# Moving the input normalisation of an attention loop from VectorE to ScalarE

## The reference

```python
x = x + tanh(g_xattn[0]) * attention(layernorm(x), ctx, ctx)   # 16 blocks of 128 tokens, 256 wide, 16 heads of 16
x = x + tanh(g_ffn[0]) * ffn(layernorm(x))                     # 32 experts x 4 sets, slots of 32 tokens

def _layernorm(x, eps=1e-05):
    m = jnp.mean(x, axis=-1, keepdims=True)
    v = jnp.var(x, axis=-1, keepdims=True)
    return (x - m) / jnp.sqrt(v + eps)
```

## Time and profile before

| | |
|---|---|
| median of three runs | 270.87 us |
| the profiled execution, in all | 272.54 us |
| its span, first to last instruction | 270.8 us |
| PE busy | 224.6 us, 83% |
| DVE busy | 199.5 us, 74% |
| ACT busy | 167.0 us, 62% |
| POOL busy | 129.2 us, 48% |
| mean granted clock of PE | 0.950 |

### The profile page before, as it was taken

One profiled execution on the slowest core, in us unless ns is written; L12 is line 12 of the kernel. 1 busy time (PEld: TensorE's weight loads), 2 busy tenths in 40 slices (PEclk: granted clock), 3 DMA queues, 4 the chain that ended last, 5 costly groups with the idle time before them and its releaser, 6 DMA issues.

```text
span 270.8 us, 7540 instructions
## 1 busy us (share of the span) xinstructions
PE 224.6 (83%) x2850; PEld 175.8 (65%) x2850; DVE 199.5 (74%) x454; ACT 167.0 (62%) x356; POOL 129.2 (48%) x243
## 2 busy tenths in 40 slices
PE   0465769499788799899989998979998999985994
PEld 0455668387576688687757676857786777773451
DVE  4786738669999969599698887789996555552573
ACT  2642648558657859778577766625887554456562
POOL 5632275555767568857586777654665000000000
PEclk9996868989999999999999999997999999997699
DMA  6735649833253442434310000007996387899724
GB/s 193 228 94 150 176 113 286 248 92 88 75 141 99 119 122 61 121 98 112 82 52 23 7 4 2 4 2 243 394 383 227 85 179 207 233 236 215 174 97 138
DMA packets 32230, 37.91 MB, mean 140 GB/s; under 512 B 4099, under 2 KB 27331, under 8 KB 31939
## 3 DMA queue, kind: packets, MB, share of 16 engines
q1 hardware_dynamic: 31763, 36.85, 47.8%
q10 hardware_dynamic: 432, 0.59, 0.9%
HBM read 18.26 MB, written 6.29 MB: 91 GB/s over the span
## 4 chain that ended last, share of the span: by engine, by line
PE 34%; DVE 19%; POOL 15%; issue 12%; DMA 8%; ACT 6%; SPq 5%; ACTq 0%; POOLq 0%; DVEq 0%
POOL pT L482 6%; PE banks L857 4%; DVE rsum L1268 4%; PE banks L931 4%; PE banks L712 4%; PE banks L732 4%; PE banks L916 3%; PE banks L754 3%; PE banks L875 3%; PE banks L603 3%; DVE nmax L1260 3%; SPq L299 2%; DMA y<-y_rows 2%; DMA w<-in_wattn_dram 2%; POOL xs L476 2%
## 5 line engine op out<-in xcount | busy, mean ns | idle before, releaser
L1260 DVE TENSOR_REDUCE nmax<-banks 128x4 f32<-128x512 f32 x64 | 43.7, 683 | 23.2 <-PE banks L666 22.9
L482 POOL TENSOR_SCALAR_AFFINE_SELECT pT<-pT 128x512 f32<-128x512 f32 x64 | 40.8, 638 | 39.3 <-ACT pT L1023 39.3
L1028 ACT ACTIVATE banks<-cb 128x512 f32<-128x512 bf16 x62 | 37.0, 597 | 12.3 <-DVE nmax L1260 12.2
L1023 ACT ACTIVATE pT<-banks 128x512 f32<-128x512 f32 x64 | 37.5, 586 | 7.5 <-PE banks L683 7.5
L683 PE MATMUL banks<-qst,kst 99*128 99x128 bf16 x256 | 25.8, 224 | 3.9 <-DMA qst<-nT 3.7
L1268 DVE RECIPROCAL rsum<-banks 128x256 f32<-128x256 f32 x16 | 28.0, 1748 | 1.3 <-PE banks L712 1.2
L712 PE MATMUL banks<-pT,va 128*32 128x128 f32 x512 | 27.4, 287 | 0.0
L666 PE MATMUL banks<-kst,qst 96*128 96x128 bf16 x256 | 25.9, 225 | 1.6 <-ACT banks L1028 1.6
L712 PE MATMUL banks<-pT,ones 128*32 128x128 f32 x512 | 25.8, 273 | 0.0
L683 PEld LDWEIGHTS banks<-qst,kst 99*128 99x128 bf16 x256 | 15.5, 100 | 9.1 <-DMA qst<-nT 3.9
L1108 ACT ACTIVATE routed<-banks 128x512 f32<-128x512 f32 x30 | 17.2, 628 | 5.3 <-PE banks L754 5.3
(11 more groups left out here) (133 smaller groups left out, 633.8 us busy)
## 6 DMA issues: line engine op xcount, KB each, us to landing
wx<-in_wexp_dram SPq DMA_DIRECT2D x32, 256.5 KB, 7.3
kst<-kp SPq DMA_DIRECT2D x48, 128.0 KB, 2.4
qst<-qp SPq DMA_DIRECT2D x48, 128.0 KB, 2.4
cT<-in_ctxT_dram SPq DMA_DIRECT2D x8, 256.0 KB, 3.4
y_rows<-ring SPq DMA_DIRECT2D x16, 128.0 KB, 3.3
y<-y_rows SPq DMA_DIRECT2D x4, 512.0 KB, 5.2
wx<-y_rows SPq DMA_DIRECT2D x4, 512.0 KB, 8.3
out_dram<-xs SPq DMA_DIRECT2D x16, 128.0 KB, 2.0
```

What stands on the lines that cost most here:

```text
L482: pool.affine_select(p, p, [[0, HC], [1, P]], ALU.is_ge, 0.0, base=0, channel_multiplier=-1)\
L1023: act.activation(pT[:, n % PR, :], BT[n % 2], ACT.Exp, scale=float(D) ** -0.5).then_inc(p_ready, 1)
L1028: act.activation(BS[n % 2], causal, ACT.Copy).then_inc(mask_placed, 1)
L1260: dve.tensor_reduce(nmax[:, b % 2, :].rearrange("p (e j o) -> p e o j", e=2, o=KH)[:, e, o], BS[n % 2].rearrange("p (j t) -> p j t", j=HC) ...
```

## The change

In the loop, DVE no longer normalises the 12 blocks 4 to 15. ACT does, in the same slots (s = 0 and 1), right behind its mask of the next chunk and ahead of its exponential. Its instruction computes `Identity(scale * x + bias)` with scale and bias read per token: the scale is the reciprocal deviation `rs`, the bias is minus mean times `rs`. DVE makes that bias for six, four and four blocks at once, with one small instruction behind each chain of deviations (`shift_x`). It is written into `ve`, which the chain no longer needs, and a new semaphore `shift_x_ready` tells ACT. The four blocks ahead of the loop and the second layernorm stay as they were.

```diff
+            def normalize_x(b):
+                act.wait_ge(shift_x_ready, 1 if b < 8 else b // 4)
+                act.wait_ge(xT_done, (b - 4) // 2 + 1)
+                act.activation(xn[:, b % 4, :], xs[:, b, :], ACT.Identity, bias=ve[:, b:b + 1], scale=rs[:, b:b + 1])\
+                    .then_inc(xn_ready, 1)
...
                 if 1 <= n < CH - 1:
                     place_mask(n + 1)
+                if s in (0, 1) and g + 2 < NG2:
+                    normalize_x(2 * (g + 2) + s)
...
-            def normalize_x(b):
-                if b >= 4:
-                    dve.wait_ge(xT_done, (b - 4) // 2 + 1)
-                normalize(b, xn_ready)
+            def shift_x(lo, hi):
+                rstd_ready(lo)
+                dve.scalar_tensor_tensor(ve[:, lo:hi], mv[:, lo:hi, 0], -1.0, rs[:, lo:hi], ALU.mult, ALU.mult)\
+                    .then_inc(shift_x_ready, 1)
...
-            normalize_x(2)
-            normalize_x(3)
+            normalize(2, xn_ready)
+            normalize(3, xn_ready)
+            shift_x(2, 8)
...
                 if n < CH:
                     row_max(n)
-                if s in (0, 1) and g + 2 < NG2:
-                    normalize_x(2 * (g + 2) + s)
                 if s == 1 and g + 2 < NG2:
                     k_rest(g + 2)
...
                     if n == first + 8:
-                        rstd_ready(lo)
+                        shift_x(lo, lo + 4)
```

More of the change, by code:

```diff
@@ L200, in build @@
         stats_ready = sem("stats_ready")
+        shift_x_ready = sem("shift_x_ready")
         tanh_ready = sem("tanh_ready")
@@ L1323, in _ @@
             rstd_ready(0)
-            normalize_x(0)
-            normalize_x(1)
+            normalize(0, xn_ready)
+            normalize(1, xn_ready)
             weight_low(Q)
```

## The result

The changed kernel takes 273.94 us (median of 19 runs, 271.86 to 276.36) against 271.33 us (19 runs, 269.55 to 273.59). The ratio is 1.0088, 95% interval 1.0062 to 1.0113, so about 2.4 us slower, 1.7 to 3.1. Every ratio in this document leaves out the runs more than 1.5% above the fastest of their kernel, which are 1 of 19 for the changed kernel but 7 of 12 in e3_copy and 7 of the 17 of the kernel before that stand beside e11 and e12, so a ratio can differ by up to 1% from what the medians of all runs say.

The account below looks back on a forecast made before the run. The prediction took a closed loop of waits through PE, DVE, ACT and POOL, 17.28 us a round, as the bound. Terms 2x - (1.63 - 2x) + 4x = 8x - 1.63, with x = 0.46, gave +2.05 us: 272.9 us, 8-in-10 range 270.3 to 274.2.

Parts of the forecast that it names:

- slower still: Rival: in round 3 masks or PE's transposes hold k_rest at its old time, nothing gained; 3.1 us slower, 274.0; chance 0.16.
- The loop through PE, ACT, DVE and POOL: Attention loop: a closed chain of waits, 17.28 us a round; a microsecond put into one link is a microsecond on the round.
- The step x: Time one added activation pushes back what follows it on ACT: 0.30 + 0.11 bias + 0.05 scale = 0.46 us, ends 0.30 and 0.52.
- Round 2: Attention loop: k_rest already waits for ACT's k_high, so the two added activations lengthen the round by 2x.
- Round 3: Attention loop: DVE came last to k_rest, so moving the normalisations gains 1.63 - 2x, with 0.28 us of ACT's delay absorbed.
- Rounds 4 and 5: Attention loop: k_rest waits for k_high, so +2x each; PE's transposes of the maxima 18.2 us apart in place of 17.28.
- Rounds 0 and 1 at nothing: Start of the loop: chain lies with SP's issues and the 4.01 us transfer of the maxima, so the added activations cost nothing.
- `shift_x` at nothing: Three small DVE bias instructions of about 0.16 us, costed at nothing under cover of other waits; 0.2 to 0.3 each if uncovered.
- PE's wait for the maxima: PE's wait before its transpose of the row maxima in rounds 4 and 5, about 1 us, was to become about 1.9 us.
- The masks: ACT's masks queued behind the new activations: PE uses them one or two slots later, so their delay stays inside that of k_high.
- The rival of the ports: Small DVE stages escape POOL's operations on the shared port pair; up to 3.4 us recovered, 269.5 us, kernel faster; chance 0.13.
- POOL and DVE move together: Argument against the port rival: the same DVE results set POOL's operations going through ACT, so the 0.06 us offset stays.

Follow-up runs that it names:

- e3_copy: Changed kernel with its twelve activations as plain copies, without scale and bias per token; ratio 0.9983 (0.9930 to 1.0035) against the kernel before.
- e11: Kernel before with ACT normalising only blocks 10 to 15, one slot before the round, ahead of the output's high part; ratio 0.9995 (0.9955 to 1.0036).
- e12: Kernel before with ACT normalising blocks 10 to 15 in its idle wait and k_high ahead of its slot's exponential and maxima copy; ratio 0.9828, median 266.79 us.
- e1: Changed kernel with ACT normalising only in rounds 4 and 5, DVE in rounds 0 to 3; ratio 1.0084 (1.0047 to 1.0120) against the kernel before.
- e4: Changed kernel with the two activations of rounds 1 to 5 moved right behind k_high on ACT; ratio 0.9944 (0.9906 to 0.9982) against the kernel before.
- e8: Changed kernel with activations behind k_high, and k_high ahead of its slot's exponential and maxima copy; ratio 0.9940 (0.9902 to 0.9979) against the kernel before.
- e10: Kernel before with k_high ahead of its slot's exponential and maxima copy, and both DVE normalisations in slot s = 0; ratio 0.9905 (0.9862 to 0.9948).
- e3b_bias: Changed kernel with the scale left out of the twelve activations, bias kept; one run, difference of medians +1.6 us against the kernel before.
- e6: Changed kernel with ACT normalising only in rounds 0 and 1, DVE in all others; ratio 1.0034 (1.0003 to 1.0066) against the kernel before.
- e9: Kernel before with only k_high taken ahead of the exponential and the copy of the maxima of its slot; ratio 0.9925 (0.9899 to 0.9951).
- e2: Changed kernel with ACT normalising only in round 3, DVE in all other rounds; ratio 0.9969 (0.9929 to 1.0008) against the kernel before.

## Why the prediction was right

The direction, the size (+2.05 forecast, about +2.4 measured) and the mechanism held. The median of 273.94 us lies inside the range of 8 in 10 but above the forecast's own range, which ended at 273.6; the kernel before was itself 0.46 us higher in this measurement (271.33 for 270.87). It is also next to the 274.0 of the rival "slower still", and there the number alone would mislead: that rival needed round 3 to gain nothing, and it gained 0.63. Point by point:

- **The loop through PE, ACT, DVE and POOL** held. e1 adds 0.98 us of ACT work to each of two rounds and they are 0.98 and 0.97 us longer. e11 adds the same work where ACT waits and it costs under 0.1. In rounds 3 to 5 the distance from `k_rest` to the next mark is 7.22 to 7.25 us in every kernel but e4, e8 and e10, so the time of such a round is set by when `k_rest` starts.
- **The step x** was the mis-sized term: 0.46 forecast, 0.49 measured. The bias was priced at 0.11 and costs 0.09; the scale was put at half of that and costs the whole 0.09. The estimate by the Trainium skill ("ScalarE: Activation LUTs", What ACT_TABLE_LOAD costs), 0.492, was the better one, and e3b_bias and e3_copy agree with its 93 ns for each operand (90 and 93). With x = 0.49 the sum is +2.29 against +2.39 by the marks.
- **Round 2** +2x: 0.92 forecast, +1.00. **Round 3** 1.63 - 2x: a gain of 0.71 forecast, 0.63; the 0.28 us that ACT was to absorb there are in the trace, where `onh` to `k_high` grew by 4.46 - 3.76 = 0.70 and not by 0.98. **Rounds 4 and 5** 18.2 us forecast, 18.29 and 18.28.
- **Rounds 0 and 1 at nothing** is not shown. e6 leaves between nothing and about 1 us for them, as said there.
- **`shift_x` at nothing** held for the last of the three, the only one between the marks. In the changed kernel it is short:

```profile
86.25 0.16 DVE L1205 SCALAR_TENSOR_TENSOR rs<-nt,rs 128x4 f32<-128x4 f32 x1
86.44 0.16 DVE L1229 SCALAR_TENSOR_TENSOR ve<-mv,rs 128x4 f32<-128x4 f32 x1
```

In e1 it is not, and there the nothing is partly luck. It took 0.55 us beside POOL's operations, and the normalisation behind it, so made later, took 0.74 in place of the 1.20 of before:

```profile
85.75 0.55 DVE L1229 SCALAR_TENSOR_TENSOR ve<-mv,rs 128x4 f32<-128x4 f32 x1
...
86.25 1.16 POOL L460 TENSOR_TENSOR qp<-qr,qp 128x512 bf16<-128x512 f32 x1
86.82 0.74 DVE L1223 TENSOR_SCALAR xn<-xs,mv,rs 128x256 f32<-128x256 f32 x1
```

- **One sign of it was wrong.** PE's wait for the maxima was to grow to about 1.9 us. It is 1.05. PE does lose the time, but it loses it earlier in the round, ahead of its transposes of x and of its projection of `onh`. Neither had a named wait in round 4 before:

```profile
107.88 0.66 PE L596 MATMUL banks<-cf,xn 128*128 128x128 f32 x4 [0.23 <-DVE kr L1246]
...
109.94 0.39 PE L626 MATMUL banks<-wh,onh 128*128 128x256 f32 x1 [0.39 <-ACT va L1016]
```

Counted from the mark, the transposes start 0.46 us later than before and the projection 0.96 us later, nearly all of the round's delay. The first waits for `k_rest`, the second for ACT's copy of the values, which also stands behind the two activations. The prediction had named neither. The masks, which it had named, did stay inside the delay of `k_high`: between the 4th and the 11th mark PE names no wait for them.

- **The rival of the ports** did not show in the changed kernel: the four slow small stages of DVE in round 2 took 1.12, 0.66, 0.58 and 1.23 us before and after. The fifth, 0.68 us at 85.08, did become 0.16 (86.25), but `k_high` came last there and nothing was gained by it. The argument against this rival, that POOL and DVE move together, is weaker than the prediction put it. In e9 moving one activation by 0.64 us separated them by 0.37 us and gave back 0.75.

## What to carry to other kernels

Before work is moved from a busy engine to a less busy one, look for the last arrival at the instruction where the two engines meet, round by round: here ACT was 62% busy overall and yet without any idle time in just the eight instructions ahead of `k_high`. The same work is nearly free where that engine's own row shows an idle wait (1.88 us ahead of `onh`; it cost 0.06 us a round in e11). And where two engines arrive together, as both did at `k_rest` in rounds 4 and 5, relieving either alone gave at most 0.06 us; the pair of edits gave 0.55.

## What the runs showed of the hardware that I had not expected

PE's granted clock fell once in the later part of the attention loop in the traces of six kernels and not in those of the other seven. Stretches of e4_behind and then of the kernel before:

```profile
134.50:136.50 2.00, 0.84 (x12) 0.45 (x8) 1.57 (x4) 2.00 (x5) 1.44 (x6) 1.00 0.04 8
136.00:138.00 2.00, 1.69 (x26) 1.07 (x24) 1.54 (x4) 1.92 (x5) 1.92 (x5) 0.72 0.49 131
138.00:140.00 2.00, 2.00 (x24) 1.39 (x23) 1.35 (x2) 1.20 (x2) 2.00 (x3) 0.50 0.03 6
```

```profile
136.00:138.00 2.00, 0.86 (x9) 0.52 (x9) 1.57 (x4) 2.00 (x5) 1.53 (x6) 1.00 0.06 15
138.00:140.00 2.00, 2.00 (x42) 1.43 (x43) 1.86 (x6) 1.84 (x5) 2.00 (x4) 1.00 0.46 124
```

0.50 is the lower level, 1.2 GHz. The half round in which it falls is 7.8 us in place of 6.92. Just ahead of the fall PE was busy for only 0.84 us of 2. But so it was at the same place of all thirteen traces (0.81 to 0.89), and the clock fell only in those of e2, e4, e6, e8, e10 and e12. What decides stays open. The fall lies behind the 11th mark, so the distances above are free of it, but it puts 0.9 us into some times and can be one reason why they spread.
